# Attention scores contracted over 64 rows instead of 128, two matmuls issued together

## The chip, the cores and the metric

One core of a Trainium2 chip runs the whole program. The metric is the time of one execution in device microseconds (us), the median of several. A profiled execution gives the trace from which all rows come. TensorE (PE) multiplies matrices into PSUM, VectorE (DVE) and ScalarE (ACT) read PSUM, GpSimd (POOL) works on SBUF only, and SyncE (SP) issues most transfers.

## The reference

The input is x, 8 batches of 512 tokens with 256 features. Two blocks follow each other, each a branch between layer norms:

```python
x = x + layernorm(attn(layernorm(x)))     # 16 heads of 16 features
x = x + layernorm(ffn(layernorm(x)))      # 256 -> 1024 -> 256, a LoRA expert per token

att = softmax(einsum('blhd,bmhd->blmh', q, k) / 4, axis=2)
opt = einsum('blmh,blhd->blhd', att, v)   # m is summed out of att alone
```

In the second einsum the index m stands in `att` only. So the output of a head is v, row by row, times the sum of that row's softmax. The kernel still computes every score: for each batch 16 heads x 4 query tiles of 128 x 512 scores, their maximum per row, the exponentials and their sum, and from these the ratio of the sum with itself.

## The kernel before, in words

Values that matmuls take are split in a high and a low fp32r half. For the scores, q.k is q_high.k_high + q_high.k_low + q_low.k_high + q_low.k_low: four products of 16 features, so 64 rows of contraction for one head. SyncE (and for the first piece GpSimd) copies q and k by DMA from `qk` into the tile `stack`. One piece of `stack` serves two heads: head p=0 in rows 0 to 63, head p=1 in rows 64 to 127. Plane 2 of a piece holds the k rows of both heads; planes 0 and 1 hold the q rows of one head each, with zeros in the other head's rows. A score matmul then contracts over all 128 rows, and the zeros take out the other head. There are 3 pieces in a ring (`PIECES`), and their zeros are written once, by three memsets on GpSimd at the start (L1084, semaphore `zeroed`).

A batch has 64 scores (two heads by four tiles by eight pieces' halves), numbered i over the whole run, 512 in all; i = 2g + p. Each goes through three engines: the matmul (PE, L227) writes bank `ps[i % NS]`, DVE takes the negated row maximum (L703), ACT computes the exponential in place and its row sum (L516). NS is 5, so score i may be computed once exponential i - 5 is done:

```python
if i >= NS:
    e.wait_ge(exped, i - NS + 1)
```

The other three banks, `pu`, serve all other matmuls: the transposes of xn, v, y (`x_t`, `o_t`, `y_t`), the projections (`q_k`, `value`, `project`), the gate (`gate`, `gate_t`, `masked_t`) and the two layers of the FFN (`f1`, `f2`). Each engine's order is written out by hand, with `slot(s)` where the next score of the batch stands: on PE slot(s) is score s + 4 of the batch, on DVE maximum s + 2, on ACT exponential s. The other work stands between the slots, for instance on PE in batches 2 to 6:

```python
slot(14), slot(15), f2(b - 2, 0, 0)
slot(16), f2(b - 2, 0, 1), x_t(b + 1, 0), slot(17), slot(18), slot(19), f2(b - 2, 1, 0), slot(20)
slot(21), f2(b - 2, 1, 1), slot(22), x_t(b + 1, 1), slot(23), slot(24), slot(25), f2(b - 2, 2, 0)
slot(26), f2(b - 2, 2, 1), slot(27), slot(28), slot(29), f2(b - 2, 3, 0), slot(30), f2(b - 2, 3, 1)
slot(31), slot(32), y_t(b - 1, 0), y_t(b - 1, 1), slot(33), q_k(b + 1, 0), slot(34), slot(35)
```

So the FFN of batch b-2, the middle of batch b-1, the scores of b and the projections of b+1 run interleaved. In batches 0 and 1 there is less other work, and `run_idle` puts a filler matmul on a tile of ones (L206) before most scores, into the same bank; the list `FULL` names the slots without one. After the last score the rest of the last batch runs by itself.

Of the kernel before, what the change touches and what calls it, by code (L numbers as in the profile page):

```python
# [6 lines left out]
F32 = mybir.dt.float32  # L7
F32R = mybir.dt.float32r
# [4 lines left out]
B, L, D, H, F, E, R = 8, 512, 256, 16, 1024, 8, 4  # L13
# [3 lines left out]
PIECES = 3  # L17
XB = 5
PAIRS = 32


IDLE, FULL = (25, 3, 4), (5, 20, 26, 31, 36, 38, 42, 46, 60, 68, 72, 75, 77, 81, 86, 87, 94, 95, 97, 100, 102, 103,
                           104, 105, 109, 110, 112, 116, 121, 126)
NS = 5
# [9 lines left out]
def sandwich(nc, x, wqk, wv, bqk, wout, wgate, wi, lora, wib, wo, bfree, bg, ident, out):  # L34
    with ExitStack() as ctx:
        def sb(name, shape, dt=F32):
            return ctx.enter_context(nc.sbuf_tensor(name, shape, dt))

        def sem(name):
            return ctx.enter_context(nc.semaphore(name))  # L40

        ps = [ctx.enter_context(nc.psum_tensor(f"ps{i}", [128, 512], F32)) for i in range(NS)]
# [4 lines left out]
        xnT = sb("xnT", [128, 2, 2, L], F32R)  # L47
        qk = sb("qk", [128, 4, 2, L], F32R)

        stack = sb("stack", [128, PIECES, 3, 2, L], F32R)  # L50
        vo = sb("vo", [128, 2, NT, D])
        oT = sb("oT", [128, 2, L])
        y = sb("y", [128, NT, D])
# [56 lines left out]
        first_stacked = [[sem(f"first_stacked{c}_{p}") for p in range(2)] for c in range(2)]  # L110
        stored = [sem(f"stored{i}") for i in range(XB)]

        const_set, zeroed = sem("const_set"), sem("zeroed")
        qk_split, v_split, wqk_high = sem("qk_split"), sem("v_split"), sem("wqk_high")
        late = sem("late")

        scored, maxed, exped = sem("scored"), sem("maxed"), sem("exped")
# [24 lines left out]
        def here(b):  # L142
            return 0 <= b < B
# [6 lines left out]
        def place(g):  # L150


            b, n = divmod(g, PAIRS)
            if b < B - 1:
                return g // 8, n % 8 // 4, n % 4
            h, i, c, t = n // 16, n % 16 // 4, n % 4 // 2, n % 2
            return 4 * b + h + i, c, 2 * h + t
# [7 lines left out]
        def pieces_at(piece):  # L165

            return 128 * (piece // PIECES + (piece % PIECES > 0))

        def first_piece(e, c, p):

            e.wait_ge(qk_low, 2 * c + 2)
            e.wait_ge(zeroed, PIECES)
            for t in range(4):
                qa, ka = t // 2, 2 + t % 2
                e.dma_start(stack[64 * p + t:64 * p + 64:4, 0, 1 - p:3:1 + p, c].bitcast(F32),
                            qk[p:128:8, qa:ka + 1:ka - qa, c].bitcast(F32)).then_inc(first_stacked[c][p], 16)


# [1 line left out]
        def tensor(e):  # L180
# [22 lines left out]
            def run_idle(bank, n):  # L203

                for _ in range(n):
                    e.matmul(bank[:].rearrange("p (k m) -> p k m", k=4), ones_r[:],  # L206
                             ones_r[:].unsqueeze(1).to_broadcast([128, 4, 128]), start=True, stop=True)

            def b_last(g):
                return g >= (B - 1) * PAIRS  # L210

            def score(i):
                g, p = divmod(i, 2)
                if g >= B * PAIRS:
                    return
                piece, c, t = place(g)
                if i in (0, 8):
                    e.wait_ge(first_stacked[c][0], 64)
                    e.wait_ge(first_stacked[c][1], 64)
                elif i % 16 == 0 or b_last(g) and i % 8 == 0:  # L220
                    e.wait_ge(stacked[piece % PIECES], pieces_at(piece))
                if i >= NS:
                    e.wait_ge(exped, i - NS + 1)
                if 4 <= i < 4 * PAIRS + 4 and i - 4 not in FULL:
                    run_idle(ps[i % NS], 1)
                st = stack[:, piece % PIECES]
                e.matmul(ps[i % NS][:], st[:, 1 - p, c, t * 128:(t + 1) * 128], st[:, 2, c, :], start=True,  # L227
                         stop=True).then_inc(scored, 1)

            def gates(out_, yt):  # L230

# [195 lines left out]
            for t in ALL:  # L427
                e.wait_ge(normed[0], t + 1)
                for c in range(2):
                    p = e.transpose(first[c][:, t * 128:(t + 1) * 128], xn[:, t, c * 128:(c + 1) * 128], id_s[:])  # L430
# [17 lines left out]
            def slot(s):  # L448
                score(2 * PAIRS * b + s + 4)
# [515 lines left out]
        def pool(e):  # L965
# [114 lines left out]
            for i in range(E):  # L1080
                e.memset(w8[:, :, i:i + 1], float(E - i)).then_inc(const_set, 1)
            e.memset(ms[:, :, 96:98], 1.0).then_inc(const_set, 1)
            for i in range(PIECES):
                e.memset(stack[:, i, 0:2].rearrange("p q c l -> p (q c l)").bitcast(F32), 0.0).then_inc(zeroed, 1)  # L1084
            e.wait_ge(const_set, CONSTS)
            e.wait_ge(rstd[0], 2)
            e.tensor_tensor(nmr[0][:, 2, :], nmr[0][:, 1, :], halves[:], ALU.pow).then_inc(rstd[0], 1)
            e.wait_ge(normed[0], 4)
            first_piece(e, 0, 1)
            first_piece(e, 1, 1)  # L1090
            x_norm(1)
            late_halves(0, [(wi_r[:, :, 0, half(i)], wi_st[:, half(i)]) for i in range(2)], wi_loaded, 16)
# [37 lines left out]
        def sync(e):  # L1130
            def load_x(b):
                if here(b):
                    if b >= XB:
                        e.wait_ge(stored[b % XB], 16 * (b // XB))
                    e.dma_start(xb[:, b % XB], x[b].rearrange("(t p) d -> p t d", p=128)).then_inc(x_loaded[b % XB], 16)

            def stacks(b, j):
                if here(b):
                    piece = 4 * b + j
                    ring = piece % PIECES  # L1140
                    e.wait_ge(qk_low, 4 * b + 4)
                    if j >= PIECES and b == B - 1:

                        e.wait_ge(scored, 2 * PAIRS * b + (8 if j == PIECES else 40))
                    elif piece >= PIECES:
                        e.wait_ge(scored, 16 * (piece - PIECES) + 16)
                    for p in range(2):
                        for t in range(4):
                            qa, ka, s = t // 2, 2 + t % 2, 2 * (j % 4) + p
                            dst = stack[64 * p + t:64 * p + 64:4, ring, 1 - p:3:1 + p].rearrange(  # L1150
                                "p q c l -> p q (c l)")
                            src = qk[s:128:8, qa:ka + 1:ka - qa].rearrange("p q c l -> p q (c l)")
                            e.dma_start(dst.bitcast(F32), src.bitcast(F32)).then_inc(stacked[ring], 16)  # L1153

            def store(b):
                if here(b):
                    e.wait_ge(added[3], 4 * b + 4)
                    e.dma_start(out[b].rearrange("(t p) d -> p t d", p=128), xb[:, b % XB]).then_inc(stored[b % XB], 16)

            for t in ALL:  # L1160
                e.dma_start(xb[:, 0, t], x[0, t * 128:(t + 1) * 128, :]).then_inc(x0_loaded[t], 16)
            e.wait_ge(wqk_loaded, 16)
            e.wait_ge(x0_loaded[NT - 1], 16)
            e.dma_start(wv_st, wv).then_inc(wv_loaded, 16)
            load_x(1)
            e.dma_start(wo_st, wo).then_inc(wo_loaded, 16)
            e.dma_start(wi_st, wi[:, 0, :]).then_inc(wi_loaded, 16)
            e.dma_start(wg_s[:], wgate).then_inc(wg_loaded, 16)
            e.dma_start(bg_s[:], bg).then_inc(bg_loaded, 16)
            e.dma_start(wout_s[:], wout).then_inc(wout_loaded, 16)  # L1170
            e.dma_start(bf[:], bfree).then_inc(bf_loaded, 16)
            first_piece(e, 0, 0)
            first_piece(e, 1, 0)
            stacks(0, 1)
            e.wait_ge(late, 4)
            e.dma_start(wi_st, wi[:, 1, :]).then_inc(wi_loaded, 16)
            e.dma_start(lst[0:96], lora).then_inc(lora_loaded, 16)
            e.dma_start(lst[96:98], wib).then_inc(lora_loaded, 16)
            stacks(0, 2)
            stacks(0, 3)  # L1180
            e.wait_ge(late, 12)
            load_x(2)
            e.wait_ge(late, 21)
            e.dma_start(lb_r[97:98].bitcast(F32), rl.bitcast(F32)).then_inc(lora_moved, 16)
            for b in range(B):
                if b:
                    stacks(b, 3)
                store(b - 3)
                if b:
                    load_x(b + 2)  # L1190
                stacks(b + 1, 0), stacks(b + 1, 1), stacks(b + 1, 2)

            stacks(B - 1, 4)
            store(B - 3), store(B - 2)
            b = B - 1
            for t in ALL:
                e.wait_ge(added[3], 4 * b + t + 1)
                e.dma_start(out[b, t * 128:(t + 1) * 128, :], xb[:, b % XB, t, :]).then_inc(tile_stored, 16)
            for i in range(XB):
                e.wait_ge(stored[i], 16 * len(range(i, B - 1, XB)))  # L1200
            e.wait_ge(tile_stored, 64)
# [68 lines left out]
```

## Time and profile before

| | us |
|---|---|
| median of 3 runs | 522.53 (522.11 to 523.46) |
| the profiled execution | 521.92 |
| its span in the trace | 520.1 |
| PE busy | 500.2 |
| DVE busy | 464.3 |
| ACT busy | 452.3 |
| POOL busy | 344.9 |

The difference between the profiled execution and its span, 1.8 us, lies around the first and the last instruction. A busy matmul is counted until its modelled end, so matmuls that follow each other overlap in the trace and PE looks fuller than its issue is. The duration of a single exponential is likewise longer than the distance between two that run back to back.

### The profile page before, as it was taken

Reading aid. Unit: us, or ns where it says so; the run is one execution under the profiler, and the core shown is the slowest. Engines: PE = TensorE matmul, PEld = TensorE weight load, DVE = VectorE, ACT = ScalarE, POOL = GpSimd, SP = SyncE. Lnnn points to the kernel's source line nnn. Section 1 sums busy time; section 2 is a strip of 40 time slices with the busy share of each in tenths; the row PEclk is TensorE's granted clock in tenths of the full one; section 3 lists DMA queues with packets and bytes.
Section 4 is the critical chain, followed back from the end, with each engine's and each line's share of the span. In section 5 each row is a group of like instructions: output and inputs, shape, how many; then the busy total and the mean of one; then the engine's idle time right before and its main releaser. Section 6 shows DMA issues by size and latency. Waiting matters only on the chain.

```text
span 520.1 us, 8924 instructions
## 1 busy us (share of the span) xinstructions
PE 500.2 (96%) x2750; PEld 410.6 (79%) x2750; DVE 464.3 (89%) x1005; ACT 452.3 (87%) x1238; POOL 344.9 (66%) x544
## 2 busy tenths in 40 slices
PE   8998989999999999999999999999999999899995
PEld 6756556788898779887898779887888788578995
DVE  5798999998999999998999999999999899984545
ACT  3699998999999999999999999999999989894230
POOL 5697048216882888658891988478873968695363
PEclk9999999999999999999999999999999999999998
DMA  6783364027310545027410644036400760310002
GB/s 230 229 206 94 81 164 122 1 67 177 78 45 2 130 114 163 1 52 192 112 52 1 160 115 132 1 89 155 122 1 7 191 169 0 83 41 1 1 1 82
DMA packets 22691, 47.63 MB, mean 92 GB/s; under 512 B 5266, under 2 KB 13586, under 8 KB 22004
## 3 DMA queue, kind: packets, MB, share of 16 engines
q1 hardware_dynamic: 21956, 45.95, 33.3%
q0 software_dynamic: 256, 0.52, 0.4%
q10 hardware_dynamic: 432, 0.59, 0.3%
q8 instruction: 22, 0.36, 0.3%
q14 instruction: 25, 0.20, 0.1%
HBM read 8.24 MB, written 4.19 MB: 24 GB/s over the span
## 4 chain that ended last, share of the span: by engine, by line
PE 43%; ACT 36%; DVE 10%; issue 3%; POOL 2%; SPq 2%; DMA 1%; POOLq 0%; ACTq 0%
ACT ps L516 26%; PE pu L199 20%; PE ps L227 9%; DVE nmax L703 6%; PE pu L296 4%; PE ps L199 4%; ACT qk L530 2%; ACT y L585 2%; PE pu L239 2%; SPq L1153 2%; DVE st L745 1%; PE ps L206 1%; ACT oT L544 1%; ACT vo L538 1%; DMA stack<-qk 1%
## 5 line engine op out<-in xcount | busy, mean ns | idle before, releaser
L516 ACT ACTIVATE ps<-ps,nmax 128x512 f32<-128x512 f32 x512 | 345.7, 719 | 12.3 <-DVE nmax L703 11.8
L703 DVE TENSOR_REDUCE nmax<-ps 128x1 f32<-128x512 f32 x512 | 319.9, 680 | 15.8 <-PE ps L227 15.6
L227 PE MATMUL ps<-stack 128*128 128x512 f32 x512 | 179.7, 415 | 1.9 <-ACT ps L516 1.7
L516 ACT ACTIVATION_READ_ACCUMULATOR ps<-ps,nmax 128x1 f32 x512 | 135.9, 265 | 0.0
L227 PEld LDWEIGHTS ps<-stack 128*128 128x128 f32 x512 | 93.8, 189 | 25.7 <-ACT ps L516 11.7
L199 PE MATMUL pu<-yT,wi_r 128*128 128x512 f32 x336 | 87.3, 395 | 0.0
L199 PEld LDWEIGHTS pu<-wo_r,inter 128*128 128x128 f32 x648 | 83.8, 188 | 3.2
L199 PE MATMUL pu<-wo_r,inter 128*128 128x256 f32 x648 | 85.5, 282 | 0.0
L199 PEld LDWEIGHTS pu<-yT,wi_r 128*128 128x128 f32 x336 | 63.3, 188 | 13.8
L206 PE MATMUL ps<-ones_r 128*128 128x512 f32 x130 | 53.6, 451 | 7.6 <-ACT ps L516 6.6
L206 PEld LDWEIGHTS ps<-ones_r 128*128 128x128 f32 x130 | 25.5, 198 | 29.5 <-ACT ps L516 22.6
L199 PE MATMUL pu<-xnT,wqk_r 128*128 128x512 f32 x186 | 47.5, 392 | 0.0
L1051 POOL TENSOR_TENSOR inter<-y,inter 128x1024 fp32r<-128x1024 f32 x19 | 45.5, 2393 | 1.5
L994 POOL TENSOR_TENSOR ml<-gs,g 128x128 f32<-128x128 f32 (+1 forms) x9 | 3.5, 388 | 64.8 <-DVE g L855 64.8
L974 POOL TENSOR_TENSOR nmr<-nmr,halves 128x2 f32<-128x2 f32 (+2 forms) x50 | 39.7, 795 | 4.2
L986 POOL TENSOR_TENSOR xb<-xb,y 128x256 f32<-128x256 f32 x58 | 41.1, 734 | 1.8
L199 PEld LDWEIGHTS pu<-xnT,wqk_r 128*128 128x128 f32 x186 | 34.9, 188 | 7.5
L1017 POOL TENSOR_TENSOR vo<-vo,sone 128x256 f32<-128x256 f32 x32 | 18.9, 622 | 27.4 <-DVE sone L806 26.2
L971 POOL TENSOR_SCALAR nmr<-mv 128x2 f32<-128x2 f32 (+2 forms) x50 | 11.9, 239 | 34.4 <-DVE mv L750 32.0
L296 PE MATMUL pu<-wout_s,oT 128*128 128x256 f32 x128 | 31.6, 382 | 2.2 <-ACT oT L544 1.7
L980 POOL TENSOR_SCALAR y<-y,nmr 128x256 f32<-128x256 f32 x58 | 31.6, 555 | 2.4
L296 PEld LDWEIGHTS pu<-wout_s,oT 128*128 128x128 f32 x128 | 23.7, 189 | 7.6 <-DVE inter L735 3.7
(167 smaller groups left out, 698.0 us busy)
## 6 DMA issues: line engine op xcount, KB each, us to landing
stack<-qk SPq DMA_DIRECT2D x256, 128.0 KB, 2.5
xb<-in_x SPq DMA_DIRECT2D x7, 512.0 KB, 3.9
out_y<-xb SPq DMA_DIRECT2D x7, 512.0 KB, 3.5
xb<-in_wo SPq DMA_DIRECT2D x1, 1024.0 KB, 7.5
vo<-in_wi SPq DMA_DIRECT2D x2, 512.0 KB, 6.5
oT<-in_wqk ACTq DMA_DIRECT2D x1, 512.0 KB, 3.8
xb<-in_x SPq DMA_DIRECT2D x4, 128.0 KB, 3.8
stack<-qk SPq DMA_DIRECT2D x8, 64.0 KB, 2.5
```

Source lines behind the costliest of these rows:

```text
L199: p = e.matmul(out_, lT(a, c), r(b_, c), start=first and n == 0 and j == 0, stop=last and n == len(chunks) - 1 and j == 2)
L206: e.matmul(bank[:].rearrange("p (k m) -> p k m", k=4), ones_r[:], ones_r[:].unsqueeze(1).to_broadcast([128, 4, 128]), start=True, stop=True)
L227: e.matmul(ps[i % NS][:], st[:, 1 - p, c, t * 128:(t + 1) * 128], st[:, 2, c, :], start=True, stop=True).then_inc(scored, 1)
L296: p = e.matmul(o, oT[:, c, t * 128:(t + 1) * 128], wout_s[:, c, :], start=c == 0, stop=c == 1)
L516: e.activation(ps[i % NS][:], ps[i % NS][:], ACT.Exp, bias=nmax[:, i % 8:i % 8 + 1], accum_out=ssum[:, b % 2, t, h:h + 1]).then_inc(exped, 1)
L703: e.tensor_reduce(nmax[:, i % 8:i % 8 + 1], ps[i % NS][:], AX_X, ALU.max, negate=True).then_inc(maxed, 1)
L971: e.tensor_scalar(nmr[n][:, 0, s], mv[n][:, s, 0], -1.0, None, ALU.mult).then_inc(rstd[i], 1)
L974: e.tensor_tensor(nmr[n][:, 2, s], nmr[n][:, 1, s], halves[:, s], ALU.pow).then_inc(rstd[i], 1)
L980: e.tensor_scalar(dst[:, t, :], src[:, t, :], nmr[n][:, 0, t:t + 1], nmr[n][:, 2, t:t + 1], ALU.add, ALU.mult).then_inc(normed[i], 1)
L986: e.tensor_tensor(xb[:, b % XB, t, :], xb[:, b % XB, t, :], src[:, t, :], ALU.add).then_inc(added[i], 1)
L1017: e.tensor_tensor(vt, vt, sone[:, t, :].unsqueeze(2).to_broadcast([128, H, 16]), ALU.mult).then_inc(scaled, 1)
L1051: e.tensor_tensor(inter[:, 1, f:f + 2, :], whole, high.bitcast(F32), ALU.subtract).then_inc(f1_pool_low, 1)
```

## The change

A score contracts over its own 64 rows: p=0 over rows 0 to 63, p=1 over rows 64 to 127, so the two matmuls of a pair use different halves of the array's rows and write different banks. `stack` loses the second q plane and the zeros, and with them go the memsets and the waits on them. On PE `score(i)` does nothing for an even i; the call for the odd i of a pair issues both matmuls, behind the wait of the odd one. The fillers of both stand ahead of both. The order of slots on all engines is as before.

```diff
-        stack = sb("stack", [128, PIECES, 3, 2, L], F32R)
+        stack = sb("stack", [128, PIECES, 2, 2, L], F32R)
...
-            e.wait_ge(zeroed, PIECES)
             for t in range(4):
                 qa, ka = t // 2, 2 + t % 2
-                e.dma_start(stack[64 * p + t:64 * p + 64:4, 0, 1 - p:3:1 + p, c].bitcast(F32),
+                e.dma_start(stack[64 * p + t:64 * p + 64:4, 0, :, c].bitcast(F32),
...
             def score(i):
-                g, p = divmod(i, 2)
-                if g >= B * PAIRS:
+                if i % 2 != 1 or i >= 2 * B * PAIRS:
                     return
+                g = i // 2
                 piece, c, t = place(g)
+                i = 2 * g
...
-                if i >= NS:
-                    e.wait_ge(exped, i - NS + 1)
-                if 4 <= i < 4 * PAIRS + 4 and i - 4 not in FULL:
-                    run_idle(ps[i % NS], 1)
+                if i + 1 >= NS:
+                    e.wait_ge(exped, i + 1 - NS + 1)
+                if 4 <= i < 4 * PAIRS + 4:
+                    for k in (i, i + 1):
+                        if k - 4 not in FULL:
+                            run_idle(ps[k % NS], 1)
                 st = stack[:, piece % PIECES]
-                e.matmul(ps[i % NS][:], st[:, 1 - p, c, t * 128:(t + 1) * 128], st[:, 2, c, :], start=True,
-                         stop=True).then_inc(scored, 1)
+                for p in range(2):
+                    rows = slice(64 * p, 64 * p + 64)
+                    e.matmul(ps[(i + p) % NS][:], st[rows, 0, c, t * 128:(t + 1) * 128], st[rows, 1, c, :], start=True,
+                             stop=True).then_inc(scored, 1)
...
-            for i in range(PIECES):
-                e.memset(stack[:, i, 0:2].rearrange("p q c l -> p (q c l)").bitcast(F32), 0.0).then_inc(zeroed, 1)
...
-                            dst = stack[64 * p + t:64 * p + 64:4, ring, 1 - p:3:1 + p].rearrange(
-                                "p q c l -> p q (c l)")
+                            dst = stack[64 * p + t:64 * p + 64:4, ring].rearrange("p q c l -> p q (c l)")
```

## Rows read from the trace of the kernel before

**Rows 1.** The page: busy time by engine, granted clock in 40 slices, chain by engine.

```profile
PE 500.2 (96%) x2750; PEld 410.6 (79%) x2750; DVE 464.3 (89%) x1005; ACT 452.3 (87%) x1238; POOL 344.9 (66%) x544
...
PEclk9999999999999999999999999999999999999998
...
PE 43%; ACT 36%; DVE 10%; issue 3%; POOL 2%; SPq 2%; DMA 1%; POOLq 0%; ACTq 0%
```

**Rows 2.** Windows, one steady batch: us, busy of PE, PEld, DVE, ACT, POOL, clock, DMA.

```profile
248.40:305.70 57.30, 56.94 (x320) 48.03 (x321) 55.27 (x121) 55.94 (x155) 41.77 (x65) 1.00 0.36 93
```

**Rows 3.** Waits, whole span: engine line waited for, total us, times, longest.

```profile
DVE nmax L703 <- PE ps L227: 15.6, 29, 1.2
...
ACT ps L516 <- DVE nmax L703: 11.8, 26, 1.3
```

**Rows 4.** Timeline of PE, the FFN's second layer: start us, us, what, merged.

```profile
254.03 1.59 PE L199 MATMUL pu<-wo_r,inter 128*128 128x256 f32 x12
255.46 0.39 PE L227 MATMUL ps<-stack 128*128 128x512 f32 x1
255.69 1.60 PE L199 MATMUL pu<-wo_r,inter 128*128 128x256 f32 x12
257.12 0.60 PE L239 MATMUL pu<-id_s,xn 128*128 128x128 f32 x4
257.48 0.96 PE L227 MATMUL ps<-stack 128*128 128x512 f32 x3
...
266.76 1.58 PE L199 MATMUL pu<-wo_r,inter 128*128 128x256 f32 x12
268.18 0.39 PE L227 MATMUL ps<-stack 128*128 128x512 f32 x1
```

**Rows 5.** Timeline of DVE, the same stretch.

```profile
254.41 3.07 DVE L703 TENSOR_REDUCE nmax<-ps 128x1 f32<-128x512 f32 x5
257.40 0.74 DVE L745 BATCH_NORM_STATS2 st<-y 128x6 f32<-128x256 f32 x2
258.18 0.25 DVE L750 BATCH_NORM_AGGREGATE mv<-st 128x2 f32<-128x6 f32 x2
...
266.16 3.14 DVE L703 TENSOR_REDUCE nmax<-ps 128x1 f32<-128x512 f32 x5
269.22 0.68 DVE L707 TENSOR_TENSOR xnT<-pu,xnT 128x512 fp32r<-128x512 f32 x1
```

**Rows 6.** Timeline of ACT, the same stretch: exponentials 19 to 21, 28, 34.

```profile
257.13 0.66 ACT L516 ACTIVATE ps<-ps,nmax 128x512 f32<-128x512 f32 x1
257.80 0.67 ACT L516 ACTIVATE ps<-ps,nmax 128x512 f32<-128x512 f32 x1
259.04 0.66 ACT L516 ACTIVATE ps<-ps,nmax 128x512 f32<-128x512 f32 x1 [0.45 <-DVE nmax L703]
...
265.32 0.68 ACT L516 ACTIVATE ps<-ps,nmax 128x512 f32<-128x512 f32 x1
...
269.54 0.67 ACT L516 ACTIVATE ps<-ps,nmax 128x512 f32<-128x512 f32 x1
```

**Rows 7.** Timeline of PE, the gate: outputs of 80 and of 40 rows.

```profile
273.74 0.40 PE L232 MATMUL pu<-yT,wg_r 128*80 128x512 f32 x1
273.97 0.40 PE L233 MATMUL pu<-yT,wg_r 128*40 128x512 f32 x1
```

**Rows 8.** Timeline of batch 0: an exponential, then the filler and score it frees.

```profile
22.46 0.65 ACT L516 ACTIVATE ps<-ps,nmax 128x512 f32<-128x512 f32 x1
...
23.28 0.19 PEld L206 LDWEIGHTS ps<-ones_r 128*128 128x128 f32 x1 [0.37 <-ACT ps L516]
...
23.62 0.39 PE L227 MATMUL ps<-stack 128*128 128x512 f32 x1
```

**Rows 9.** Timeline of POOL at the start.

```profile
1.19 5.29 POOL L1084 MEMSET stack<- 128x2048 f32 x3
7.20 1.39 POOL L1087 TENSOR_TENSOR nmr<-nmr,halves 128x4 f32<-128x4 f32 x1 [0.72 <-DVE nmr L886]
```

More of the change, by code:

```diff
@@ L111, in sandwich @@
         stored = [sem(f"stored{i}") for i in range(XB)]
-        const_set, zeroed = sem("const_set"), sem("zeroed")
+        const_set = sem("const_set")
         qk_split, v_split, wqk_high = sem("qk_split"), sem("v_split"), sem("wqk_high")
```

## The prediction

> **What bounds the kernel now.** I read the page first. By busy time PE looks like the bound: 96% of the span, 43% of the chain that ended last, with ACT at 36% [rows 1]. A change that halves the array time of 512 matmuls looks large from there. The windows of one steady batch correct this. Of 57.30 us ACT is busy for 55.94, DVE for 55.27 and PE for 56.94 [rows 2], and PE's figure is inflated, since a score matmul is counted for 0.39 us while the next matmul starts 0.23 us after it (255.46 to 255.69) [rows 4]. All three engines are nearly full, and ACT cannot be relieved by this change. What could be won is the time in which ACT stands still for want of a score: it waits 11.8 us in all for a maximum, and DVE 15.6 us in all for a score [rows 3]. So the most that the change can give is about 12 us of 522, however cheap the matmuls become. What it can lose has no such cap. Its second half, the moved issue of the even scores, is the part that I cost in detail.
>
> **How the ring works.** Back to back, exponentials start 0.67 us apart (257.13, 257.80) [rows 6], maxima 0.60 us apart (five from 254.41 to 257.40) [rows 5]. In batch 0 an exponential that starts at 22.46 lets the next matmul load at 23.28: 0.82 us from start to release. Its filler and score follow, and the score starts 0.34 and lands 0.73 us after the release (24.01) [rows 8]. Score i needs exponential i - 5 done. From the start of that exponential to the turn of exponential i there are 5 x 0.665 = 3.33 us. The chain takes 0.82 + 0.73 + 0.68 for the maximum (0.61 to 0.69 in the rows, and a handover) + 0.05 = 2.28 us with a filler: slack about 1.0 us. This slack lets DVE and PE do a piece of other work between scores without ACT noticing.
>
> **Memsets, waits and layout: 0.** The three memsets fill POOL from 1.19 to 6.48 us. The next instruction there starts at 7.20, after 0.72 us of waiting for DVE [rows 9], so the wait for statistics covers them; without that cover they would cost up to 5.29 us once. DMAs have the same number, bytes and queue; only destination planes change. The sequence on SP is unchanged.
>
> **The matmul pair on PE: gain 0.2 us a pair where PE is the bound, nothing elsewhere.** The trace has no matmul over 64 rows. Bounds for a pair's issue: 0.235 us if the two run side by side, 2 x 0.235 = 0.47 us if they do not, as now. Above that, if the array must empty before its rows are divided differently, the difference between length and distance of a matmul, 0.39 - 0.235 = 0.16 us, twice a pair (fillers and f1, f2 use all rows): 0.235 + 0.32 = 0.56 us. The nearest row is the gate: matmuls with 80 and 40 output rows follow each other 0.23 us apart (273.74, 273.97) [rows 7], so changing the used part of the columns costs nothing. I take 0.25. The Trainium skill ("TensorEngine Tiling (Array Packing)", Key Properties) speaks against the change here: changing the tiling mode drains TensorE. By the gate's rows a pair saves 0.2 us; by that rule it loses 0.1. No row here divides the rows of the array, so the trace neither bears the rule out nor refutes it; the drain is a rival below, worked from rows.
>
> **The later even score: the loss.** Two things delay it. First, it now waits for the odd score's exponential, one later. Its budget shrinks to 4 x 0.665 = 2.66 us. With two fillers ahead the chain is 0.82 + (0.73 + 0.235) + 0.68 + 0.05 = 2.52 us: in batches 0 and 1 the slack is 0.14 instead of 1.0 us. Alone this costs nothing, but each interruption on DVE now shows on ACT.
>
> Second, where other work stands between an even and an odd slot, the even score moves behind it. In batches 2 to 6 that is the case for slots 4, 16, 22, 26, 30, 32, 40, 44, 46 and 62: ten of 32. Queued behind it are everything that follows on DVE and ACT, in strict order. I follow the two worst.
>
> Slot 16 (score 20). Now it stands between f2(0,0) and f2(0,1) at 255.46; its maximum is the last of the five from 254.41, so at 256.8, and its exponential starts at 257.80 [rows 4 to 6]. After the change both f2 blocks (1.43 us each, from 254.03) and the transposes (0.36 us) go first. The pair starts at 254.03 + 2.86 + 0.36 = 257.25 and lands at 257.7, the maximum ends near 258.35, and exponential 20 starts at 258.45: 0.65 late. Behind maximum 20 stand the statistics of y (257.40 to 258.43 together [rows 5]), which move by 0.95; maximum 21 and exponential 21 move with them, from 259.04 to 260.0. That is 0.95 us more of ACT standing still. PE has gained 0.23 us in this place, and it buys nothing.
>
> Slot 30 (score 34). It stands at 268.18, its maximum at 266.16 + 4 x 0.61 = 268.6, its exponential at 269.54. With 0.95 us of lateness carried, pair (32,33) waits for exponential 28, which starts at 265.32 + 0.95 and is done 0.85 later, at 267.1; f2(3,0) starts at 267.4, the two blocks end at 270.3, and the pair lands at 270.7. The turn of maximum 34 is 268.6 + 0.95 = 269.55, so it is 1.15 late, and exponential 34, due at 269.54 + 0.95 = 270.5, starts at 271.4: 0.85 more. Slot 26 between them is the same double block, but there ACT has two transposes to copy, and the same count gives about 0.1.
>
> The other seven move by one block of 0.4 to 2.4 us, and each meets a queue at DVE. I take 0.3 us for them together; bounds are 0 and 7 x 0.95 = 6.7. Sum for a steady batch: 0.95 + 0.85 + 0.1 + 0.3 = 2.2 us. It is not won back later, since ACT has only 57.30 - 55.94 = 1.4 us of idle time by count [rows 2].
>
> **The sum.** Batches 2 to 6: 5 x 2.2 = 11.0. Batch 0 has two such even slots (4, 30) and batch 1 ten, all with single blocks and ACT with less other work: 0.5 and 1.0. The last batch has eleven, one of them behind two f2 blocks (slot 14): 1.5. Together 14.0. Against the profiled execution 521.9 + 14.0 = 535.9; the median of the runs lies 0.6 above that execution, so 536.5 us. The work after the last exponential is not touched. The forecast's own range is 529 to 543, from two thirds of a loss of 14 downwards to half of it more upwards.
>
> **Rivals.**
> *Relief of PE (faster).* In the f2 stretch, from 254.03 to past 268.18 [rows 4], PE hardly stops, and the chain's largest share is PE [rows 1]. Eight pairs in it save 8 x 0.22 = 1.8 us. If the late even scores are caught by the queue at DVE, ACT's waits for a maximum halve: 522.5 - 5.9 = 516.6. It decides if maximum 20 is less than about 0.3 us late. For it: PE's share of the chain. Against it: the working of slots 16 and 30. Chance 0.18.
> *Both small.* Losses and relief cancel: 522.5. Chance 0.08.
> *Drain.* Each division and return costs 0.16 us. A pair takes 0.56 instead of 0.47 us: 9 pairs in the f2 stretch add 0.8 us a batch, and scores that land late do so by 0.16 more in some five places: 1.5 a batch, 12 in all, on top of the forecast: 548. This is the way of the Trainium skill's rule named above. For it: nothing in the rows. Against: the gate's distance of 0.23. Chance 0.16.
> *No side by side.* The change's promise fails, the pair takes 0.47. The odd score lands 0.235 later in about three places a batch, 0.7 x 7 = 5: 541. Chance 0.06.
> *Clock.* The granted clock is 2.4 GHz (9s on the page) through all scores [rows 1]; less matmul work in batches 0 and 1 might lose it. At 1.2 GHz the 0.97 us from release to landing would near 1.9, and a loop over two pairs be 0.8 over its budget, 0.4 us a pair for some 60 pairs: 24 more, above 555. No row of the stages with scores shows the lower level. Chance 0.02.
>
> **How the numbers follow.** Forecast 0.50; the others as given; sum 1.00. The likeliest is 536.5. The range 518 to 549 leaves out most of the relief case (0.14) and the top of drain, uncosted even slots and clock (0.06). A measurement of this kernel tells about 0.3% from no change. Slower: 0.50 + 0.16 + 0.06 + 0.02 = 0.74; same 0.08; faster 0.18.
>
> **What would show it.** In the trace after: exponential 21 and 34 of a steady batch each with an idle time before them, and a period of about 59.5 us in place of 57.3; ACT's waits for a maximum up from 11.8 to about 25 us; DVE waiting for scores after f2 pairs. The two matmuls of a pair start within some tens of ns (side by side) or 0.23 us apart (not). A pair after f2 that starts 0.16 us later than the distance of f2 matmuls shows the drain. POOL's first wait grows by 5.3 us and nothing else at the start moves. The prediction is wrong if maximum 20 keeps its time: then the queue at DVE was deeper than I count, or PE arrives much earlier at the block than 254.03.

## The result and the profile after

The changed kernel takes 566.71 us (563.77 to 568.29, 4 runs) against 522.47 us, a ratio of 1.0837 (95% interval 1.0789 to 1.0885): 44 us slower, where 14 were forecast. The direction was right; the size was three times too small, and the time lies outside the range. Two executions of one kernel below, single_64, its profiled one among them, ran more than 1.5% longer than its fastest and are left out of its time and ratio.

The page after (busy time by engine, the group of the exponentials):

```profile
PE 521.5 (92%) x2750; PEld 365.7 (65%) x2750; DVE 468.5 (83%) x1005; ACT 461.2 (82%) x1238; POOL 339.4 (60%) x541
...
L521 ACT ACTIVATE ps<-ps,nmax 128x512 f32<-128x512 f32 x512 | 340.0, 668 | 45.4 <-DVE nmax L708 42.9
```

ACT now waits 42.9 us for maxima, where it waited 11.8 [rows 3]; its share of the span fell from 87% [rows 1] to 82%. ACT runs the same 1238 instructions; it is the standing still that grew. The waits of the whole span name the next step of the chain:

```profile
DVE nmax L708 <- PE ps L232: 57.3, 75, 3.5
PEld ps L232 <- issue: 45.8, 127, 1.0
```

DVE waits for scores 57.3 us (15.6 before). The second row is new: 127 times the weight load of a score (PEld) waits, 45.8 us in all, for nothing that the profile shows, which it calls "issue". One steady batch, from one ratio of sums (DVE RECIPROCAL) to the next, by windows (us, PE, PEld, DVE, ACT, POOL, clock, DMA):

```profile
269.80:332.40 62.60, 59.04 (x322) 41.73 (x321) 55.76 (x121) 57.02 (x155) 41.74 (x64) 1.00 0.31 83
```

62.6 us in place of 57.3 [rows 2]. The starts of these reciprocals divide the run. Each column gives the length of a batch in the profiled execution, in us (batch 0 from the span's start; "steady" is each of batches 3 to 5):

| kernel | batch 0 | 1 | 2 | steady | 6 | 7 | rest | span |
|---|---|---|---|---|---|---|---|---|
| before | 69.3 | 57.6 | 58.0 | 57.3 | 55.8 | 58.3 | 49.2 | 520.1 |
| changed | 74.3 | 69.0 | 63.9 | 62.6 | 60.5 | 60.8 | 49.1 | 565.5 |
| pair_128_two_waits | 71.1 | 59.1 | 61.2 | 60.5 | 58.8 | 59.0 | 49.2 | 539.8 |
| pair_128 | 73.2 | 59.7 | 62.3 | 61.3 | 59.3 | 59.1 | 49.3 | 546.7 |
| pair_64_3planes | 74.4 | 65.3 | 64.0 | 62.6 | 60.5 | 60.9 | 49.2 | 562.2 |

The rest, after the last score, kept its 49.2 us, as forecast. The stretch that the prediction followed, on ACT after (exponentials 19 to 21 and 34; rows between them left out):

```profile
285.45 0.67 ACT L521 ACTIVATE ps<-ps,nmax 128x512 f32<-128x512 f32 x1
...
286.89 0.66 ACT L521 ACTIVATE ps<-ps,nmax 128x512 f32<-128x512 f32 x1 [0.66 <-DVE nmax L708]
...
288.41 0.66 ACT L521 ACTIVATE ps<-ps,nmax 128x512 f32<-128x512 f32 x1 [0.74 <-DVE nmax L708]
...
300.36 0.66 ACT L521 ACTIVATE ps<-ps,nmax 128x512 f32<-128x512 f32 x1 [1.34 <-DVE nmax L708]
```

From exponential 19 to 21 it is 2.96 us, before 1.91 (257.13 to 259.04) [rows 6]: 1.05 more, where 0.95 was forecast. From 21 to 34 it is 11.95 us, before 10.50 (259.04 to 269.54): 1.45 more, 0.85 plus 0.1 forecast. PE and its weight loads in the same stretch:

```profile
286.30 1.69 PE L198 MATMUL pu<-wo_r,inter 128*128 128x256 f32 x12
...
287.91 0.18 PEld L232 LDWEIGHTS ps<-stack 64*128 64x128 f32 x2
287.91 0.49 PE L232 MATMUL ps<-stack 64*128 64x512 f32 x2
...
288.34 1.48 PEld L198 LDWEIGHTS pu<-wo_r,inter 128*128 128x128 f32 x12 [0.24 <-issue]
```

Two loads within 0.18 us and two matmuls within 0.49, the mean length of one (490 ns on the page): the pair does run side by side. But from one f2 block's start to the next it is 2.04 us (286.30 to 288.34), while a block with a single score took 1.66 (254.03 to 255.69) [rows 4]. A block of twelve is 1.43, so the pair takes 0.61 us, more than two single scores at 0.235 each.

### The profile page after: what moved, and what is told of

It reads as the page before. It is cut to its first block, busy times and chain, and to the rows that moved or that the text cites. A ratio compares the mean times of both kernels' runs of the same rounds, so it can differ in the third digit from the quotient of the medians.

```text
span 565.5 us, 8918 instructions
## 1 busy us (share of the span) xinstructions
PE 521.5 (92%) x2750; PEld 365.7 (65%) x2750; DVE 468.5 (83%) x1005; ACT 461.2 (82%) x1238; POOL 339.4 (60%) x541
## 4 chain that ended last, share of the span: by engine, by line
PE 56%; DVE 22%; ACT 16%; POOL 3%; issue 2%; DMA 1%; SPq 0%; POOLq 0%; ACTq 0%; DVEq 0%
PE pu L198 27%; ACT ps L521 13%; DVE nmax L708 12%; PE ps L232 10%; PE pu L301 5%; PE ps L198 3%; PE ps L205 3%; DVE st L750 3%; POOL vo L1022 2%; PE pu L244 2%; PE pu L346 1%; DVE yT L712 1%; PE pu L325 1%; ACT xnT L527 1%; DVE mv L755 1%
## 5 line engine op out<-in xcount | busy, mean ns | idle before, releaser
L521 ACT ACTIVATE ps<-ps,nmax 128x512 f32<-128x512 f32 x512 | 340.0, 668 | 45.4 <-DVE nmax L708 42.9
L708 DVE TENSOR_REDUCE nmax<-ps 128x1 f32<-128x512 f32 x512 | 323.9, 680 | 58.1 <-PE ps L232 57.3
L232 PE MATMUL ps<-stack 64*128 64x512 f32 x512 | 121.4, 490 | 8.7 <-ACT ps L521 8.5
L521 ACT ACTIVATION_READ_ACCUMULATOR ps<-ps,nmax 128x1 f32 x512 | 108.4, 212 | 0.0
L232 PEld LDWEIGHTS ps<-stack 64*128 64x128 f32 x512 | 46.7, 185 | 74.9 <-issue 45.8
L198 PE MATMUL pu<-yT,wi_r 128*128 128x512 f32 x336 | 92.4, 410 | 0.0
L198 PEld LDWEIGHTS pu<-wo_r,inter 128*128 128x128 f32 x648 | 79.1, 188 | 9.3 <-issue 7.7
L198 PEld LDWEIGHTS pu<-yT,wi_r 128*128 128x128 f32 x336 | 59.4, 188 | 23.5 <-issue 11.3
L205 PE MATMUL ps<-ones_r 128*128 128x512 f32 x130 | 49.5, 467 | 13.8 <-ACT ps L521 12.6
L198 PE MATMUL pu<-xnT,wqk_r 128*128 128x512 f32 x186 | 51.9, 419 | 0.5
```

Of the source, the lines that this page charges most:

```text
L198: p = e.matmul(out_, lT(a, c), r(b_, c), start=first and n == 0 and j == 0, stop=last and n == len(chunks) - 1 and j == 2)
L232: e.matmul(ps[(i + p) % NS][:], st[rows, 0, c, t * 128:(t + 1) * 128], st[rows, 1, c, :], start=True, stop=True).then_inc(scored, 1)
L521: e.activation(ps[i % NS][:], ps[i % NS][:], ACT.Exp, bias=nmax[:, i % 8:i % 8 + 1], accum_out=ssum[:, b % 2, t, h:h + 1]).then_inc(exped, 1)
L708: e.tensor_reduce(nmax[:, i % 8:i % 8 + 1], ps[i % NS][:], AX_X, ALU.max, negate=True).then_inc(maxed, 1)
```

## The experiments

All stand on the kernel before with its tile of three planes, except where the changed kernel is named. Ratios are to the kernel before on the same chip.

**pair_128: the order alone.** The changed `score`, with the 128-row matmuls and the zeros of before.

```diff
-                e.matmul(ps[i % NS][:], st[:, 1 - p, c, ...], st[:, 2, c, :], ...)   # arguments cut at ...
+                for p in range(2):
+                    e.matmul(ps[(i + p) % NS][:], st[:, 1 - p, c, ...], st[:, 2, c, :], ...)
```

> The scores of a pair issued together at the odd slot, behind the odd score's wait, but each still over all 128 rows with the zeros. Theory A (the late even score, my forecast's mechanism): this alone costs about 14 us plus up to 5 for the two matmuls that run one after the other, 536 to 541 us. Theory B (dividing the rows of the array is the whole loss): the order costs nothing, 522 to 524 us, and the loss appears only over 64 rows. Theory C (the granted clock of batches 0 and 1): here the array works as much as before, so the clock stays at 2.4 GHz and the batches 0 and 1 lose under 2 us each.

548.08 us, ratio 1.0498 (1.0455 to 1.0542). The order costs 26 us by itself: the mechanism of the forecast, at nearly twice its size and above the 536 to 541 us expected. Theory B, that the division is the whole loss, falls. Theory C expected full clock and under 2 us lost in each of batches 0 and 1: they lost 3.9 and 2.1 (table), with a mean clock of 0.97 from 22 to 74 us.

**single_64: 64 rows at the old places.** As before, with `rows = slice(64 * p, 64 * p + 64)` in the matmul.

> Every score at its own slot and behind its own wait as before, but over its own 64 rows. Theory B (each change between 64 and 128 rows empties the array, about 0.15 to 0.2 us each way): more changes than with pairs, since a score that stands alone between two other blocks pays both ways, so at least 560 us. Theory A (late even scores): none is late here, so 520 to 525 us.

608.14 and 615.12 us, ratio 1.1711 (1.1626 to 1.1797): 89 us slower, with no score moved and no wait changed, as theory B expected (at least 560). So 64 rows without pairs cost far more than the whole change. In the profile the mean granted clock from 20 to 140 us was 0.69, and batches 0 and 1 took 96.9 and 98.3 us; a steady batch, at full clock, took 63.5, 6.2 more than before and 0.9 more than with the change. So most of the loss lies in the first two batches, where a filler over 128 rows stands ahead of most scores; how much of it is the division and how much the clock stays open.

**pair_64_3planes: the changed order and rows on the old tile.**

> The changed kernel's pairs over 64 rows on the old tile of three planes, with the memsets, the wait on them and the old destinations of the transfers. If tile, memsets and destinations count nothing, 564 to 568 us as the changed kernel; if the removal of the memsets or the adjacent planes matter, more than 2 us away from it.

563.47 us, ratio 1.0796 (1.0765 to 1.0828). The interval overlaps that of the changed kernel (the time itself falls just under the 564 to 568 us expected), and from batch 2 on every batch has the same length (table). The profiled executions differ in batch 1 alone, 65.3 against 69.0, with a mean clock of 0.95 against 0.88 from 74 to 144 us. The single executions of both kernels lie on one line of time against mean clock (566.04 us at 0.983 and 563.77 at 0.989 of the changed kernel, 565.66 at 0.983 and 564.02 at 0.990 here). So planes, memsets and destinations show no effect that these runs tell from no effect.

**probe_rows: the distances themselves.** Behind the first fillers, on the tile of ones.

```diff
+            for _ in range(4):
+                half_rows(2)             # rows 0-63, then 64-127
+                run_idle(ps[2], 2)       # two over 128 rows
+            half_rows(12)
+            run_idle(ps[2], 12)
...
+            for k in range(8):           # eight over rows 0-63
+                e.matmul(ps[3][:]..., ones_r[0:64], ones_r[0:64]..., start=True, stop=True)
```

> The kernel before with a row of test matmuls of 512 columns on the tile of ones behind the first fillers: four times (two over 64 rows in the two halves, two over 128 rows), then twelve over 64 rows in alternating halves, twelve over 128 rows, four times (one over 64 rows, two over 128), and eight over the same 64 rows. Theory B: the first matmul after each change starts 0.35 to 0.45 us after the last one before it, in place of 0.235; twelve in alternating halves take six distances of 0.235. If the array does not empty: 0.235 at each change.

The timeline of PE of this kernel (one execution, 536.57 us with the test matmuls in it):

```profile
9.45 0.74 PE L206 MATMUL ps<-ones_r 128*128 128x512 f32 x2
10.11 0.49 PE L429 MATMUL ps<-ones_r 64*128 64x512 f32 x2
10.54 0.73 PE L206 MATMUL ps<-ones_r 128*128 128x512 f32 x2
...
13.37 1.65 PE L429 MATMUL ps<-ones_r 64*128 64x512 f32 x12
14.96 3.04 PE L206 MATMUL ps<-ones_r 128*128 128x512 f32 x12
...
22.24 2.12 PE L441 MATMUL ps<-ones_r 64*128 64x512 f32 x8
24.29 1.09 PE L448 MATMUL pu<-id_s,xn 128*128 128x128 f32 x8
```

From two full matmuls to the next two full ones it is 1.09 us (9.45 to 10.54). Two full ones and one pair side by side make 3 x 0.235 = 0.705; the remaining 0.385 is two changes of the division, 0.19 us each. The start distances across a change are 0.43 us (10.11 to 10.54), as theory B had it. Twelve in alternating halves take 1.59 us, 6 x 0.235 + 0.18; eight in the same half take 2.05, 8 x 0.235 + 0.17, so only different halves run together. The kernel's other series, one matmul over 64 rows and two over 128, repeats every 1.08 us (17.92 to 19.00): a lone matmul over 64 rows costs as much as a lone pair. A lone pair costs 0.62 us against 0.47 for two full matmuls. Worked out from these numbers, n pairs in a row cost 0.235 n + 0.385 against 0.47 n, so they would only win from two in a row. On the weight loads one sees what happens:

```profile
10.11 0.19 PEld L429 LDWEIGHTS ps<-ones_r 64*128 64x128 f32 x2 [0.37 <-issue]
10.54 0.30 PEld L206 LDWEIGHTS ps<-ones_r 128*128 128x128 f32 x2 [0.24 <-issue]
```

Between full matmuls the loads run under the matmuls (eight loads from 6.87 us on, while ten matmuls run from 6.63 to 9.08). At a change the load is not pulled ahead under the running matmul: it starts at 10.11, 0.08 us before the modelled end of the two full ones (9.45 + 0.74), and at the same time as its own matmul. The profile calls the 0.37 and 0.24 us before it "issue". Most of the 127 waits of the changed kernel, 0.36 us each in the mean, are of this kind: the same order over 128 rows (pair_128) has 11 such waits.

```profile
PEld ps L231 <- issue: 6.1, 11, 1.0
```

The rule of the Trainium skill ("TensorEngine Tiling (Array Packing)", Key Properties), that changing the mode drains TensorE, holds here at 0.19 us a change.

**pair_128_two_waits and pair_128_early: place or wait.** The first issues both at the odd slot, each behind its own wait and filler. The second issues both at the even slot behind the odd one's wait. Both over 128 rows.

```diff
                 for p in range(2):
+                    if i + p >= NS:
+                        e.wait_ge(exped, i + p - NS + 1)
```

> Both scores over 128 rows at the odd slot, but each behind its own wait and filler as in the kernel before. If the one wait makes the loss of the odd-slot pairs, this is at 522 to 530 us; if the moved place makes it, 542 to 548 us. In batches 0 and 1 (two fillers ahead, shorter budget) it should win back most of their 6 us in either case.

> Both scores of a pair over 128 rows, issued at the even slot instead of the odd one, behind the odd score's wait: no score moves behind other work, but the work that stood between the two slots now waits for the odd score's exponential. If the place behind other work is what makes the 26 us of the 128-row pairs at the odd slot, this one takes 522 to 530 us. If it is the one wait for both (the even score one exponential later), it stays above 540 us.

Two waits: 540.67 us, ratio 1.0348 (1.0329 to 1.0366). Neither expected range holds it, but it lies next to the one for the moved place. The place costs 18 us, the one wait 7 to 8 more (548.08), of which the table puts 0.8 in a steady batch and 2.0 in batch 0. In batches 0 and 1 the step also moves the fillers (two ahead of both, against one ahead of each), and batch 0 is not measured that finely: in late_others below, where it is issued as before, it took 71.7 us against 69.3. Of the 5.9 us that pair_128 lost in batches 0 and 1, two waits won back 2.7, not most of it.

Early: 557.49 us, ratio 1.0665 (1.0646 to 1.0684). My expectation failed: the loss does not go when no score stands behind other work. A steady batch is 61.6 us, and the weight loads of scores wait 36.1 us for an exponential, against 15.9 in pair_128. While they wait, the work behind them on PE waits too. Counted as in the table of exponentials below, batch 4 is 1.6 us late by exponential 8 and 0.4 to 0.6 us more each by 25, 34, 37, 43 and 52, so this is a loss at many places. Both scores at the even slot behind two separate waits were not run for whole batches.

**pair_64_early: the same place over 64 rows.**

> The 64-row pairs at the even slot. With the even scores no longer late what is left is the change of the array's division, 0.15 us a pair beyond the two single matmuls by the probe (1.09 - 0.47 - 0.47), and what it does to batches 0 and 1. If loss of place and of division add, 14 to 20 us above the 128-row pairs at the even slot, and the steady batch 1.3 us above theirs.

579.35 us, ratio 1.1084 (1.1046 to 1.1122): 22 us above its 128-row kin, a little over what was expected; the steady batch is 63.0, 1.4 above 61.6, as expected. Most of the rest lies in batches 0, 1 and the last.

**late_16_30 and late_others: which slots.** The kernel before, with only chosen even scores moved to the next odd slot, in batches 2 to 6.

```diff
+            def deferred(i):
+                b_, s = divmod(i - 4, 2 * PAIRS)
+                return i % 2 == 0 and 2 <= b_ <= 6 and s in (16, 30)
```

> The kernel before, with only the even scores of slots 16 and 30 moved to the next odd slot, in batches 2 to 6, with their own waits and over 128 rows. These are the two places that the prediction worked out, at 0.95 and 0.85 us. If that working holds, each of the five batches takes 1.8 us more: 531.3 us. If the place costs mostly elsewhere: under 526 us.

> The same for the other eight even slots with work behind them (4, 22, 26, 32, 40, 44, 46, 62) in batches 2 to 6. The prediction gave them 0.4 us a batch together: 524.3 us. The two-waits kernel loses 3.2 us in a steady batch; if the eight hold what the two do not, 1.4 us a batch: 529 us.

Slots 16 and 30: 533.47 us, ratio 1.0205 (1.0190 to 1.0220), 10.7 us for five batches, 2.1 each (59.4 against 57.3 in the profile), where the worked-out loss was 1.8. ACT in that kernel, exponentials 19 to 21:

```profile
261.88 0.66 ACT L527 ACTIVATE ps<-ps,nmax 128x512 f32<-128x512 f32 x1
263.23 0.66 ACT L527 ACTIVATE ps<-ps,nmax 128x512 f32<-128x512 f32 x1 [0.57 <-DVE nmax L714]
264.75 0.66 ACT L527 ACTIVATE ps<-ps,nmax 128x512 f32<-128x512 f32 x1 [0.74 <-DVE nmax L714]
```

2.87 us from 19 to 21, 0.96 more than before: the forecast's 0.95. At exponential 34 another 0.98 is lost, where 0.85 was forecast, and 0.2 more by exponential 37. The other eight: 530.72 us, ratio 1.0141 (1.0124 to 1.0158), 7.4 us, 1.3 to 1.5 a batch (58.6 in the profile). The prediction had 0.4 for them. The parts add: 2.1 + 1.3 = 3.4 against 3.2 for all ten with two waits.

Where in a batch the time is lost can be read from the starts of the exponentials. The table gives the start of exponential s of batch 4, counted from exponential 0 of that batch, less the same in the kernel before (us; 64 is the first of the next batch):

| kernel | 8 | 15 | 21 | 30 | 37 | 44 | 64 |
|---|---|---|---|---|---|---|---|
| late_16_30 | 0.01 | 0.01 | 0.97 | 0.95 | 2.13 | 2.13 | 2.13 |
| late_others | 0.00 | 0.67 | 0.67 | 0.65 | 0.57 | 1.25 | 1.37 |
| pair_128_two_waits | 0.01 | 0.69 | 1.29 | 1.26 | 2.48 | 3.16 | 3.27 |
| mixed_128 (below) | 0.02 | 0.69 | 0.69 | 1.27 | 1.41 | 2.10 | 2.22 |
| pair_128 | 0.30 | 0.97 | 1.75 | 1.73 | 3.24 | 3.93 | 4.05 |
| changed | 0.53 | 1.29 | 2.35 | 2.33 | 3.99 | 4.86 | 5.39 |

Batches 3 and 5 agree within about 0.1. Of the eight other slots two make nearly the whole loss: slot 4 (score 8, moved behind a block of f1 and two transposes; 0.67 by exponential 15) and slot 40 (score 44, moved behind `gate_t` and `value`; 0.68). The other six, slot 26 among them, cost about nothing.

**pair_64_from_2: batches 0 and 1 left alone.**

> The 64-row pairs at the odd slot in batches 2 to 7 only, with batches 0 and 1 issued as in the kernel before. Five batches at 5.3 us more, the last at 5.9 with its tail: about 555 us if the change's cost in each batch is independent; then batches 0 and 1 make 8 to 12 of the 41 to 44 us of the whole change, by the array's division between fillers and pairs and by the clock, which stays at 2.4 GHz here.

552.74 us, ratio 1.0573 (1.0552 to 1.0594). Batches 0 and 1 thus carry 12 us (against the pairs on the old tile, 1.0796) to 14 us (against the changed kernel, 1.0837), at and above the upper end of what was expected.

**mixed_128: a mended order.** Pairs with two waits at the odd slot, but at the even slot for 16, 26 and 30, in batches 2 to 6.

> Pairs over 128 rows with their own two waits in batches 2 to 6 only, at the odd slot except for slots 16, 26 and 30, where both scores go to the even slot, between the two blocks of the second FFN layer. There ACT runs dry and banks are free, so the odd score's wait should not hold the block. If the two long gaps without a score make the loss, a steady batch falls from 60.5 to about 58.5 us and the total is 527 to 530 us; if the many small moves make it, 535 us or more.

533.63 us, ratio 1.0211 (1.0196 to 1.0226). A steady batch is 59.4 us, 1.1 less than with two waits at the odd slot everywhere (60.5). It missed the expected 527 to 530 us. The table of exponentials shows why: the early place does undo the loss at slots 16 (0.00 from 15 to 21, where two waits lose 0.60) and 30 (0.14 from 30 to 37, where they lose 1.22). But from 21 to 30 it loses 0.58, where two waits lose nothing; slot 26, which cost nothing late, now has its pair early there, though these runs do not tell which early pair costs it. The rest is slots 4 and 40, which were left late. An order with only slots 16 and 30 early, and slots 4 and 40 as before, was not run.

**after_more_fill, after_fill_64, after_no_fill, before_no_fill: the clock of batches 0 and 1.** The changed kernel with one filler more ahead of each pair, with its fillers over 64 rows, and without fillers; and the kernel before without them.

> The changed kernel with one more filler ahead of each pair in batches 0 and 1. Theory C (the lost clock in batch 1 is worth 5 to 9 us and comes from less matmul work): the granted clock stays at 2.4 GHz and batch 1 falls from 69 to below 64 us in spite of the longer way to the scores; total 559 to 563 us. If the clock is not the cause, the extra fillers only lengthen the loop, 0.12 us a pair or more, and it is at 570 us or above.

> The changed kernel with its fillers over 64 rows as well, in the half of their bank's score, so that nothing in the array's division changes between filler and pair and two fillers run side by side. If the division made the extra cost of batches 0 and 1 and the clock holds, batch 1 takes 60 to 62 us and the total 556 to 560 us. If it is the clock, which such fillers keep busy for less time, it falls further and the total is 570 us or more.

> The changed kernel without any filler before scores. The clock should fall to half in long stretches of batches 0 and 1; if that costs more than the fillers, batch 1 is above 70 us and the total above 572 us; if the fillers' length and division are the cost, it is below 563 us.

> The kernel before without fillers before scores. Same question in the order without pairs: if the clock falls, batches 0 and 1 take 5 us or more longer (528 us and above); if slack covers a half clock, within 2 us of 522.

569.29 us (ratio 1.0903, 1.0885 to 1.0921), 565.85 (1.0837, 1.0819 to 1.0855), 564.86 (1.0821, 1.0803 to 1.0839) and 524.80 (1.0045, 1.0030 to 1.0061). None of the four falls inside a range that was expected for it. From batch 2 on the three variants of the changed kernel have its lengths within 0.3 us, but for the last batch without fillers (62.4 against 60.8). Batches 0 and 1, with the mean granted clock of two windows:

| kernel | batch 0 | batch 1 | clock 22 to 74 us | clock 74 to 144 us |
|---|---|---|---|---|
| before | 69.3 | 57.6 | 1.00 | 1.00 |
| before_no_fill | 70.4 | 58.0 | 0.85 | 0.94 |
| pair_128 | 73.2 | 59.7 | 0.97 | 1.00 |
| changed | 74.3 | 69.0 | 0.97 | 0.88 |
| after_more_fill | 76.9 | 67.8 | 1.00 | 1.00 |
| after_fill_64 | 75.6 | 66.1 | 0.78 | 0.87 |
| after_no_fill | 73.8 | 63.1 | 0.74 | 0.85 |

The table is of one execution each. That of after_no_fill was the shortest of its four (562.30 us, median 564.86), and by ratio this kernel and the changed one are not told apart. The windows show where the changed kernel ran at the lower level of 1.2 GHz (us, PE, PEld, DVE, ACT, POOL, clock, DMA); in the slice before, PE was busy for 2.80 of 4 us:

```profile
72.00:76.00 4.00, 2.80 (x11) 1.11 (x10) 3.38 (x8) 4.00 (x13) 0.76 (x2) 0.98 0.80 210
76.00:80.00 4.00, 3.87 (x13) 2.68 (x13) 3.97 (x12) 2.77 (x8) 2.26 (x6) 0.50 0.65 166
```

The forecasts of theory C do not fit. With the clock held at 2.4 GHz by one more filler, batch 1 is 67.8 us, not below 64, and the total 2.6 us above the changed kernel. With less clock and no fillers at all batch 1 is the shortest of the four, 63.1. So batches 0 and 1 stay dear at full clock too, and what a filler gives back in clock it takes in length ahead of the pair. The clock is not without a price, though. Over the eight executions of the changed kernel and of pair_64_3planes, with the same fillers and pairs, the time falls from 568.29 to 562.76 us as the mean clock of the run rises from 0.977 to 0.993. So about 5 us go with the clock; whether a low clock makes such a run long, or a stall that makes it long also lowers the clock, they do not show. In the kernel before the same fillers are worth 2.3 us (0.45%). The release of one pair in batch 0 of the changed kernel shows the length:

```profile
30.18 0.30 PEld L205 LDWEIGHTS ps<-ones_r 128*128 128x128 f32 x2 [0.80 <-ACT ps L521]
...
30.84 0.50 PE L232 MATMUL ps<-stack 64*128 64x512 f32 x2
```

From release to landing it is 1.16 us (30.18 to 31.34), 0.97 in the forecast, and the 0.19 between them is one change of the division. The forecast's chain of 2.52 us would thus become 2.71, over the budget of 2.66 (an estimate from this one pair). How much of batch 1's 63 to 69 us is this loop and how much the clock in single stretches stays open; the four kernels bound it but do not split it.

## Why the prediction was wrong

**Right.** The limit was read rightly as a chain of full engines in strict order, with a loss that has no cap. Whether relief of PE by itself would win anything no run shows. Memsets, waits on zeros and layout show no effect; POOL's first wait grew from 0.72 to 6.01 us, by the 5.29 of the memsets, as forecast. The two matmuls of a pair run side by side. The rest after the last score is unchanged. The mechanism (even score late, DVE and ACT behind it) is the largest part, and the walk through slots 16 and 30 held within a fifth: 2.1 us a batch against 1.8, with 0.96 against 0.95 at exponential 21 and 0.98 against 0.85 at 34.

**Wrong, by terms of the sum.** A steady batch lost 5.3 us, not 2.2:

| term | forecast | measured | by |
|---|---|---|---|
| slots 16 and 30 | 1.8 | 2.1 | late_16_30 |
| the other eight even slots | 0.4 | 1.3 | late_others |
| one wait for both, by itself | 0 | 0.8 | pair_128 - two_waits |
| the array's division | 0 (pair at 0.25 us) | 1.3 | pair_64_3planes - pair_128 |

The four measured terms add to 5.5 us; together they cost 5.3.

1. *"The other seven ... I take 0.3 us for them together."* This was a guess, with bounds 0 and 6.7, and the lower end was taken with the words that each meets a queue at DVE. With slot 26 the eight had 0.4 and cost 1.3. That each moves "by one block" was misread: slot 4 moves behind three blocks and slot 40 behind two, and these two cost 0.7 each. The other six do cost nothing, so following four slots instead of two would have found nearly all of the loss of place.
2. *"Alone this costs nothing"*, of the budget of 2.66 us. The slack was counted in a loop without other work, and the sentence's second half, that each interruption on DVE now shows, got no price. The wait for the odd score's exponential cost 7 to 8 us in all. In a steady batch it is 0.8, and that at three places where a score already stands behind other work: 0.3 by exponential 8, 0.2 more by 21 and 0.3 by 37 (pair_128 less two_waits).
3. *"I take 0.25"* for the pair. It is 0.62 with both changes. The row chosen as nearest, the gate with fewer output rows, concerns the array's columns and says nothing of its rows. The rule of the Trainium skill ("TensorEngine Tiling (Array Packing)", Key Properties), that changing the tiling mode drains TensorE, spoke against the change, the price from this kernel's own rows (0.16 us a change, 0.19 measured) was in the prediction, and a chance of 0.16 was too low for it. The rival's 1.5 us a batch is near the 1.3 measured.
4. *Batches 0 and 1, 1.5 us together.* The changed kernel lost 16.4 there (143.3 against 126.9), of which the order makes 5.9 (pair_128). A loop with 0.14 us of slack was left at nothing although a rival with 0.16 to 0.19 us in that very loop stood beside it. Drain and clock were given as separate rivals, each on top of the forecast; in batches 0 and 1 they came together. The clock did fall, but not at the price of 24 us that was put on it: about 5 us go with it.
5. *The last batch, 1.5 us*: 2.5 in the profile, and batches 2 and 6 lost 5.9 and 4.7.

So the total divides, by the ratios, in some 18 us for the place of the even scores, 8 for the one wait, and 16 to 18 for 64 rows, of which 8 to 9 fall after batch 1. Each is the cost of one more step on top of the last; taken alone at the old places, 64 rows cost 89 (single_64). None of the kernels tried beats the kernel before. A group of one pair cannot win by the probe's numbers, and in the f2 stretch hardly two pairs stand in a row.

## What to carry to other kernels

In a chain of full engines with hand-set order, what moving a producer costs is decided at a few places: here four of ten made nearly all of it, each between 0.7 and 1.2 us, and six cost nothing. Read at each place how much work the producer moves behind, and give slack that shrinks a price. A narrower matmul pays only if enough of them stand in a row: in the probe two changes of the array's row division cost 0.385 us, and a pair side by side saves 0.235. When the trace has no row for an operation, a row that differs in the very property in question is no bound, and a rule with a mechanism deserves more chance than that.

## What the runs showed that I had not expected

A load of weights is not pulled ahead across a change of the division, and the profile marks this wait as "issue". Single 64-row matmuls at the old places (single_64) cost 89 us, twice the whole change, with a mean clock of 0.69 of full from 20 to 140 us. Behind one shared wait, both scores at the even slot were worse than both at the odd slot (557.5 against 548.1 us). And the fillers, which look necessary by the granted clock, are worth only 0.45% in the kernel before.
